# The experts' first layer in three fp32r products per weight tile, transposed as it is computed

## What is computed

```python
logits = xf @ gate_w + gate_b
top_w, top_i = jax.lax.top_k(logits, K)              # E, K, HID = 8, 2, 1024
gw = jax.nn.softmax(top_w, axis=-1)
combine = (gw[:, :, None] * jax.nn.one_hot(top_i, E)).sum(axis=1)
for e in range(E):
    h = jax.nn.gelu(xf @ w1[e] + b1[e], approximate=False)
    out = out + combine[:, e:e + 1] * (h @ w2[e] + b2[e])
shared = jax.nn.gelu(xf @ ws1 + bs1, approximate=False) @ ws2 + bs2
```

## Time and profile before

| | us |
|---|---|
| median of 3 runs | 805.07 (804.23 to 806.89) |
| the profiled execution | 804.36 |
| its span, first to last instruction | 802.6 |
| PE busy in the span | 742.9 (93%) |
| ACT, DVE, POOL busy | 331.6, 405.8, 218.7 |
| first hidden of the experts to the end of the last output | 460.8 to 778.2 |

### The profile page before, as it was taken

How to read it: one execution, slowest core, us unless ns; L and a number is a source line. 1 busy time by engine, 2 the same in 40 slices (tenths; PEclk the granted TensorE clock), 3 DMA queues, 4 the chain that set the end, 5 groups by cost and what they waited for, 6 DMA issues and landing times. The chain is left out here.

```text
span 802.6 us, 14818 instructions
## 1 busy us (share of the span) xinstructions
PE 742.9 (93%) x4804; PEld 563.6 (70%) x4805; DVE 405.8 (51%) x807; ACT 331.6 (41%) x885; POOL 218.7 (27%) x217
## 2 busy tenths in 40 slices
PE   6689999999999999999999899999999999999960
PEld 5567666967696766669999856767676767676740
DVE  3767788787879766667875321212121212121214
ACT  1232556456636654463332124343434343434324
POOL 5762212151214103002078201212121212121223
PEclk9987999999999999999999999999999999999985
DMA  9952331405050713032133499412121212121216
GB/s 289 250 152 54 56 110 40 84 27 148 0 108 0 226 29 55 7 134 88 63 114 112 95 318 311 96 27 40 26 39 26 39 26 39 26 39 26 27 15 215
DMA packets 60489, 71.76 MB, mean 89 GB/s; under 512 B 15264, under 2 KB 49952, under 8 KB 59552
## 3 DMA queue, kind: packets, MB, share of 16 engines
q1 hardware_dynamic: 47968, 57.03, 25.8%
q0 software_dynamic: 7152, 9.34, 7.1%
q10 hardware_dynamic: 5328, 4.85, 2.2%
HBM read 45.57 MB, written 25.11 MB: 88 GB/s over the span
## 5 line engine op out<-in xcount | busy, mean ns | idle before, releaser
L815 ACT ACTIVATE hT<-ps,b1T 128x128 f32<-128x128 f32 x312 | 84.8, 383 | 167.2 <-PE ps L1820 167.1
L1829 PE MATMUL ps<-we,hT 128*128 x624 | 142.9, 383 | 2.5 <-ACT hT L815 2.5
L1809 PE MATMUL ps<-we,xT 128*128 x312 | 140.5, 593 | 0.3 <-issue 0.3
L1829 PEld LDWEIGHTS ps<-we,hT 128*128 128x128 f32 x624 | 117.0, 192 | 17.6 <-issue 3.2
L1330 DVE COPY hp<-ps 128x512 f32<-128x512 f32 x78 | 50.3, 686 | 146.5 <-PE ps L1809 146.5
L1103 DVE TENSOR_REDUCE mx<-ps 128x4 f32<-128x512 f32 (+1 forms) x128 | 103.6, 819 | 20.6 <-PE ps L1627 19.4
L1809 PEld LDWEIGHTS ps<-we,xT 128*128 128x128 f32 x312 | 56.3, 191 | 56.4 <-issue 56.4
L726 ACT ACTIVATE pT<-ps 128x256 f32<-128x256 f32 x128 | 49.1, 384 | 69.7 <-PE ps L1643 59.5
L1627 PE MATMUL ps<-k_stack,q_stack 96*128 96x256 f32 (+1 forms) x256 | 72.3, 368 | 5.2 <-DVE mx L1103 3.0
L592 POOL CAST yidx<-meta 128x1 int32<-128x1 f32 x39 | 7.2, 184 | 234.8 <-ACT yw L824 234.8
L597 POOL DMA_INDIRECT row_sum<-yw,yidx x39 | 60.9, 1560 | 30.5 <-issue 26.4
(11 more groups left out here) (238 smaller groups left out, 1083.7 us busy)
## 6 DMA issues: line engine op xcount, KB each, us to landing
we<-in_w SPq DMA_DIRECT2D x16, 1024.0 KB, 8.9
k_stack<-k_rows SPq DMA_DIRECT2D x24, 256.0 KB, 4.8
slot_rows<-attn SPq DMA_DIRECT2D x1, 4992.0 KB, 24.5
xs<-slot_rows ACTq DMA_DIRECT2D x37, 128.0 KB, 2.0
k_rows<-k_s SPq DMA_DIRECT2D x16, 256.0 KB, 2.1
q_stack<-q_rows SPq DMA_DIRECT2D x48, 64.0 KB, 5.6
x_raw<-in_xT SPq DMA_DIRECT2D x4, 512.0 KB, 5.1
XW<-in_x SPq DMA_DIRECT2D x4, 512.0 KB, 8.5
```

The lines of the kernel that those rows point to most:

```text
L815: last = nc.scalar.activation(hT[:, c, :], ps[:, 4 + c // 4, (c % 4) * P:(c % 4 + 1) * P], ACT.Gelu, bias=b1T[:, bass.ds(e * NH + c, 1)])
L1809: m = nc.tensor.matmul(ps[:, 2 + c, :], xT[:, q, k, :], w[:, bass.ds(e, 1), k * HID + c * 512:k * HID + (c + 1) * 512].rearrange("p o n -> ...
L1829: m = nc.tensor.matmul(ps[:, 6, 0:D], hT[:, c, :], w[:, bass.ds(e, 1), KD * HID + c * D:KD * HID + (c + 1) * D].rearrange("p o n -> p (o n)"),
```

## The change

Hidden is turned round: chunks of the expert's weights stand (128 hidden units at a time), the tokens move, and the result comes out with hidden units as rows, as `gelu` needs it. Each of 8 chunks x 2 k takes the three fp32r products of `mm3`, of 128 columns each. `h_out`, `hp` and `turn_h` are gone. The high and low parts of the weights are made anew for each tile: `high` on ACT (2 copies of 128x1024) and `low` on DVE (2 differences of 128x1024), into one of two fixed homes by the tile's parity, three tiles ahead. The tokens get a low part too (`x_lo` on DVE). The result goes to banks 2 and 3 or 4 and 5 by parity, and `hT` is double. `home_even` lies over the raw shared weights, `home_odd` over `XW`; so `shared_y` moves to a ring of two chunks (`KEPT`), X is added ahead of the result (`y_in`), SP stores chunk 5 ahead of its wait for the scatters, and POOL stores the last chunk itself. The diff, cut:

```diff
+KEPT = 2
...
+        over = ExitStack()
+        home_odd = sb("home_odd", [P, 2, KD * HID], FR, over)
+        over.close()
...
+        home_even = sb("home_even", [P, 2, KD * HID], FR, over)
+        over.close()
         ws = sb("ws", [P, EW], F, mo)
...
-        xT = sb("xT", [P, 2, KD, P], F, mo)
-        hp = sb("hp", [P, HID], F, mo)
-        hT = sb("hT", [P, NH, P], F, mo)
+        sb("xT_was", [P, 2, KD, P], F, mo)
+        hT = sb("hT", [P, 2, NH, P], F, mo)
         ysum = sb("ysum", [P, 2, D], F, mo)
         yw = sb("yw", [P, 2, D], F, mo)
-        shared_y = ws[:, :].rearrange("p (t d) -> p t d", d=D)
         yidx = sb("yidx", [P, 2, 1], I32, mo)
...
+        xT = sb("xT", [P, 2, 2, KD, P], FR, mo)
+        shared_y = sb("shared_y", [P, 2 * KEPT, D], F, mo)
...
             def rows_kept(c):
                 sp.wait_ge(s["sy_out"], c + 1)
                 sp.dma_start(row_sum[bass.ts(c, CT), :].rearrange("(n p) d -> p n d", p=P),
-                             shared_y[:, bass.ds(2 * c, 2), :]).then_inc(s["kept_out"], 16)
-
-            for c in range(CHUNKS - 3):
+                             shared_y[:, 2 * (c % KEPT):2 * (c % KEPT) + 2, :]).then_inc(s["kept_out"], 16)
+
+            for c in range(CHUNKS - 2):
                 rows_kept(c)
             for q in range(4):
                 sp.wait_ge(st_sent[q], 16 * 2 * T // P // 4)
             for q in range(2):
                 sp.dma_start(xs[:, q, :], slot_rows[q * P:(q + 1) * P, 0:D]).then_inc(xs_in[q], 16)
             sp.dma_start(meta[:, :, :], slot_rows[:, D:].rearrange("(i p) m -> p i m", p=P)).then_inc(s["meta_in"], 16)
-            rows_kept(CHUNKS - 3)
             rows_kept(CHUNKS - 2)
             sp.wait_ge(s["sy_ps"], CHUNKS)
             for e in range(EARLY, E):
                 if e % EARLY == 0:
                     sp.wait_ge(s["we_in"], 32 * e)
                 load_expert(e)
-                if e == EARLY:
-                    rows_kept(CHUNKS - 1)
 
             for q in range(2):
                 sp.wait_ge(yw_sent[q], 16 * ((TILES + 1 - q) // 2))
...
-            pool.wait_ge(s["kept_out"], 16 * CHUNKS)
+            pool.wait_ge(s["sy_out"], CHUNKS)
+            pool.dma_start(row_sum[(CHUNKS - 1) * CT:CHUNKS * CT, :].rearrange("(n p) d -> p n d", p=P),
+                           shared_y[:, 2 * ((CHUNKS - 1) % KEPT):2 * ((CHUNKS - 1) % KEPT) + 2, :]).then_inc(s["last_kept"], 16)
+            pool.wait_ge(s["kept_out"], 16 * (CHUNKS - 1))
+            pool.wait_ge(s["last_kept"], 16)
...
                     if reused:
                         act.wait_ge(s["h_ps"], t - 1)
                     act.wait_ge(s["xT_ps"], t + 1)
-                    copy(xT[:, q, :, :], ps[:, 7 * q, 0:KD * P].rearrange("p (k t) -> p k t", k=KD), "xT_out")
+                    copy(xT[:, q, 0, :, :], ps[:, 7 * q, 0:KD * P].rearrange("p (k t) -> p k t", k=KD), "xT_out")
...
 
+                def high(t, q):
+
+                    e = table_expert(t) - 1
+                    if isinstance(t, int) and t < 2:
+                        if t:
+                            for st in st_sent:
+                                act.wait_ge(st, 16 * 2 * T // P // 4)
+                            act.wait_ge(s["sy_sum"], CHUNKS)
+                        else:
+                            act.wait_ge(s["ws_split"], 4)
+                    else:
+                        act.wait_ge(s["h_ps"], t - 1)
+                    act.wait_ge(s["we_in"], (e // EARLY) * (32 * EARLY) + 32 * EARLY)
+                    for k in range(KD):
+                        cols = slice(k * HID, (k + 1) * HID)
+                        copy((home_even, home_odd)[q][:, 0, cols],
+                             we[:, bass.ds(e, 1), cols].rearrange("p o n -> p (o n)"), "w_hi")
+
                 def gelu(t, q):
                     e = table_expert(t)
-                    act.wait_ge(s["hT_ps"], t + 1)
+                    act.wait_ge(s["h_ps"], t + 1)
+                    if not (isinstance(t, int) and t < 2):
+                        act.wait_ge(s["y_ps"], t - 1)
                     for c in range(NH):
-                        last = nc.scalar.activation(hT[:, c, :], ps[:, 4 + c // 4, (c % 4) * P:(c % 4 + 1) * P],
+                        last = nc.scalar.activation(hT[:, q, c, :], ps[:, 2 + 2 * q + c // 4, (c % 4) * P:(c % 4 + 1) * P],
                                                     ACT.Gelu, bias=b1T[:, bass.ds(e * NH + c, 1)])
                     last.then_inc(s["hT_out"], 1)
...
                         x_out(t + 2, q)
                     if not isinstance(t, int) or t + 1 < TILES:
                         gelu(t + 1, 1 - q)
+                    if not isinstance(t, int) or t + 3 < TILES:
+                        high(t + 3, 1 - q)
                     weight(t, q)
 
+                high(0, 0)
+                high(1, 1)
                 x_out(0, 0, False)
                 x_out(1, 1, False)
                 gelu(0, 0)
+                high(2, 0)
                 step(0, 0)
                 step(1, 1)
...
 
+            def kept_rows(c):
+                return shared_y[:, 2 * (c % KEPT):2 * (c % KEPT) + 2, :]
+
+            def y_in(c):
+                if c:
+                    dve.wait_ge(s["kept_out"], 16 * min(c, CHUNKS - 2))
+                nc.vector.tensor_tensor(kept_rows(c), X[:, 2 * c:2 * c + 2, :], b2b[:, 0:1, :].broadcast_to([P, 2, D]), ALU.add)\
+                    .then_inc(s["sy_sum"], 1)
+
             def y_out(c):
                 dve.wait_ge(s["sy_ps"], c + 1)
-                rows = shared_y[:, 2 * c:2 * c + 2, :]
-                nc.vector.tensor_tensor(rows, ps[:, Y_BANK[c], :].rearrange("p (n d) -> p n d", n=2),
-                                        b2b[:, 0:1, :].broadcast_to([P, 2, D]), ALU.add).then_inc(s["sy_sum"], 1)
                 dve.wait_ge(s["sy_sum"], c + 1)
-                nc.vector.tensor_tensor(rows, rows, X[:, 2 * c:2 * c + 2, :], ALU.add).then_inc(s["sy_out"], 1)
+                nc.vector.tensor_tensor(kept_rows(c), ps[:, Y_BANK[c], :].rearrange("p (n d) -> p n d", n=2),
+                                        kept_rows(c), ALU.add).then_inc(s["sy_out"], 1)
 
...
+            y_in(0)
             y_out(0)
...
+            y_in(1)
             y_out(1)
...
                     x_split(c + 2)
+                y_in(c - 1)
+                if c == CHUNKS - 1:
+                    y_in(c)
                 y_out(c - 1)
 
             def expert_tiles(table_expert):
-                def h_out(t):
-                    dve.wait_ge(s["h_ps"], t + 1)
-                    if not (isinstance(t, int) and t == 0):
-                        dve.wait_ge(s["hT_ps"], t)
-                    for c in range(2):
-                        last = nc.vector.tensor_copy(hp[:, c * 512:(c + 1) * 512], ps[:, 2 + c, :])
-                    last.then_inc(s["h_out"], 1)
+                def x_lo(t, q):
+                    dve.wait_ge(s["xT_out"], t + 1)
+                    lo_of(xT[:, q, 1, :, :], ps[:, 7 * q, 0:KD * P].rearrange("p (k t) -> p k t", k=KD),
+                          xT[:, q, 0, :, :], "xT_lo")
+
+                def low(t, q):
+                    e = table_expert(t) - 1
+                    home = (home_even, home_odd)[q]
+                    for k in range(KD):
+                        cols = slice(k * HID, (k + 1) * HID)
+                        dve.wait_ge(s["w_hi"], 2 * t + k + 1)
+                        lo_of(home[:, 1, cols], we[:, bass.ds(e, 1), cols].rearrange("p o n -> p (o n)"),
+                              home[:, 0, cols], "w_lo")
 
...
+                low(0, 0)
+                low(1, 1)
+                x_lo(0, 0)
+                x_lo(1, 1)
                 y_out(CHUNKS - 1)
-                h_out(0)
+                low(2, 0)
                 for t in range(2):
-                    h_out(t + 1)
+                    x_lo(t + 2, t)
                     y_sum(t, t, False)
+                    low(t + 3, 1 - t)
                 with dve.Fori(1, 1 + LOOPS) as i:
                     for q in range(2):
-                        h_out(2 * i + q + 1)
-                        y_sum(2 * i + q, q, True)
+                        t = 2 * i + q
+                        x_lo(t + 2, q)
+                        y_sum(t, q, True)
+                        low(t + 3, 1 - q)
                 for t in range(REST, TILES):
-                    if t + 1 < TILES:
-                        h_out(t + 1)
+                    if t + 2 < TILES:
+                        x_lo(t + 2, t % 2)
                     y_sum(t, t % 2, True)
+                    if t + 3 < TILES:
+                        low(t + 3, 1 - t % 2)
...
             def shared_output(c):
                 if c >= 2:
-                    pe.wait_ge(s["sy_sum"], c - 1)
+                    pe.wait_ge(s["sy_out"], c - 1)
...
                     if not (isinstance(t, int) and t < 2):
-                        pe.wait_ge(s["xT_out"], t - 1)
+                        pe.wait_ge(s["xT_lo"], t - 1)
...
```

(87 more changed lines are left out.)

## The result

The changed kernel takes 850.48 us (four runs: 851.52, 849.58, 840.06, 851.38) where the kernel before takes 805.59 beside it: a ratio of 1.0531, 95% interval 1.0493 to 1.057. It is slower, as forecast, and the 850.5 lies in the range of 828 to 860; the forecast was 841.5, so 9 us are missing from the sum. The profiled execution is one of 851.52, span 849.8.

The account below looks back on a forecast made before the run. PE alone was taken to set the pace of the expert tiles, 7.983 us each. Start +1.3, tiles +39.5 and end -4.1 sum to +36.7 us on 804.36, 841.1 (841.8 against the median), stated as 841.5; range 828 to 860.

Parts of the forecast that it names:

- p: Pace of one weight load and 128-column product in hidden, taken as 0.112 us; 48 per tile, break-even at 0.092.
- 0.067 (the load hides): In every tile's hidden, loads go in behind the running product: total -47.6, 757.5 us; chance 0.09.
- 0.120: In hidden, the 256-column pace is the floor of a load and product pair: +51.6, 856.7 us; chance 0.10.
- The tiles: From output(0) to output(37), 37 steps of 1.068 us more each: +39.5 us.
- Splits and new waits: In the tile loop, ACT's and DVE's added work and the ring's new waits cost nothing, a tile taking 9.05 us.
- The start: Ahead of hidden(0), DVE's added work costs 0; from hidden(0) to output(0) 10.97 us instead of 9.66, +1.3.
- a limit of 0.4 for the chain: Ahead of hidden(0), DVE's sums, differences and x_lo stay covered unless they take over 0.4 us more.
- the clock falls in hidden: PE waiting on loads lowers the clock and outputs' 3.45 us double; in all tiles 135 more, 976; chance 0.03.
- the prediction's own signs of being wrong: In the tiles: p not 0.11, PE waiting for DVE's w_lo, or the clock's row under 1.00.
- The end: Last two outputs: gap of 1.16 us saves 2.35, last product at full clock 1.78 more, together -4.1 us.
- The sum: Whole kernel: 1.3 + 39.5 - 4.1 = +36.7 us, so 841.1 for the profiled execution, 841.8 against the median.
- the range's upper end: Whole kernel: 860 us, taking in the 0.120 case and a mild ring wait.

Follow-up runs that it names:

- after_again: The changed kernel unaltered, run again on another chip: 877.14 us, 1.0609 of the kernel before.
- no_split: Changed kernel with the weights' high and low parts made for tiles 0 and 1 only, later tiles reusing them: 880.35 us, single run.
- fp32_stand: Changed kernel with one plain fp32 product in place of three fp32r ones, no low parts: 770.34 us, 0.9553 of the kernel before.
- tokens_stand: Changed kernel with tokens standing and weights moving, h's copy and transposes back, x_lo ahead of low(1): 804.56 us, ratio 0.971; again 776.51, 0.9627.

## Why the prediction was right, and where it was short

- **p.** Taken as 0.112, measured 0.112 from load to load, and 9.007 us a tile against 9.05. (Within the tile, output to hidden takes 3.27 where 3.45 was put, and hidden 5.50 where 5.38 was put; behind another hidden it takes the 5.38.) It came from the loads ahead of one-column products and behind the mask; the mask's next matmul, noted 0.06 later, was indeed no pace. The rivals of p, 0.067 (the load hides) and 0.120, both fall. The Trainium skill's rule for a load ("TensorE: Matmul & The Clock Gate", section "LDWEIGHTS (loading the stationary operand)"), 107 ns for 128 columns, is within 5% of this at full clock; its 81 ns for sustained pairs at 128 columns (section "Back-to-back issue gap") does not hold for these four-byte weights, which take 112.
- **The tiles.** +39.5 forecast from output(0) to output(37). Measured: (816.35 - 481.05) - (765.64 - 470.48) = +40.1, of which 2.3 is the first step's clock (11.30 us instead of 9.01). Without it +37.8, 1.7 under the forecast, which is the 0.04 a tile of the point above.
- **Splits and new waits cost nothing.** Right: without the splits a tile takes 9.006.
- **The start** is the step that failed. "All of it ends behind the last shared output ... so hidden(0) still starts at 460.5 to 460.9. I put 0 there." DVE's chain itself was reckoned well: 7.7 us from its last split of h (452.75) to x_lo's end (460.4), measured 462.4 - 455.7 = 6.7. But I set it against PE's end in the trace before, where the last shared output starts 0.7 us behind that split's end and is drawn out to 7.04 us by a lower clock. In the changed kernel it starts 0.8 ahead of the split's end (454.85 against 455.68) and takes 6.00: 2.6 us less cover, and the chain stuck out by 1.7. Most of that is not the change's doing. The whole shared expert runs 2.9 us later in this execution, and 2.2 of these are there from the first attention stage on: the transposes that start at 30.00 in the kernel before start at 32.17, while `after_again`, the same program, has them at 30.48. PE made up for part of it, since its wait for the token rows shrank from 2.30 to 0.94. DVE's chain moved by all of it (452.75 to 455.68). I had named a limit of 0.4 for the chain, and priced what lies beyond at itself. The runs show that a gap of 1.7 there costs 11.5 in the trace, 1.7 for itself and 9.8 for the clock behind it; between medians, where the gap is 2.2, it is 10.5.
- From hidden(0) to output(0) the forecast was 10.97; it took 18.52 in the profiled execution and 10.98 where the gap was closed.
- **The clock.** The prediction gave "the clock falls in hidden" 0.03, and held "full clock all through the attention stages" against it. That was a misreading: the trace of the kernel before has a granted clock of 0.84 from 40 to 60 us and 0.75 from 60 to 80. The clock did fall, in the hiddens of tiles 0 and 1 only, and so met one of the prediction's own signs of being wrong.
- **The end.** The gap forecast at 1.16 was 1.00, and the clock stayed up: 821.02 - 816.35 = 4.67 between the last outputs where 4.62 was forecast, and 3.72 for the last. Right, in size too.
- **The sum.** 841.1 for the profiled execution, measured 851.5. The 10.4 between them are +1.7 for the gap, +7.5 to output(0), +0.6 in the tiles (+2.3 of clock, -1.7 of pace), and some +0.6 at the end and behind it. That the median of 850.5 still lies in the range is partly luck: the range's upper end stood for p = 0.120, which did not come true, and not for a fall of the clock. The third run of the changed kernel took 840.06, at a mean clock of 0.974 where the others have 0.959 to 0.962. That fits an execution without the fall; its trace was not kept, so this is argued, not shown.

## What to carry to other kernels

Count weight loads before columns: at full clock a 128x128 load of four-byte weights took 0.112 us whether 128 or 64 columns followed, so three fp32r products with 128 columns each (0.336) cost more than the one plain fp32 product of two passes (0.224). Give each load 256 to 512 columns (0.120 and 0.239 a pair here), or let the product be the plain one. And where a change puts new work of another engine between two dense stretches of PE, reckon the gap against PE's own earliest time, not against a trace in which PE was held up. With 128-column products behind it, a gap of 1.7 us cost 11.5.

## What the runs showed of the hardware

- The weight load follows the granted clock: 0.112 us a load at 2.4 GHz, 0.21 at 1.2 GHz.
- With 64 columns behind each load the granted clock was 0.81 in the mean over the tiles, in a PE that never idled; with 128 it was 1.00. Behind a gap of some 2 us it fell with 128 columns, and stayed up in the one trace with 256. Once down in two hiddens in a row, it came back only in the first output product, some 20 us later; in the kernel before it fell too, at about 452.5 at the end of the gap of 2.30 (its last shared output took 7.04 us instead of 5.92), and was back at 1.00 from 456 on.
- POOL's one-column copy of the row numbers takes six times as long when it falls into DVE's forming of differences from SBUF. In the changed kernel the copy at 606.57 lasts until 607.72, and DVE's two differences from 605.31 until 607.67. The rows of the copy, first of the kernel before, then of the changed one, then of `no_split`:

```profile
L592 POOL CAST yidx<-meta x39: 184/184/187, 477.8 to 779.2; 128x1 int32<-128x1 f32 x39
```

```profile
L599 POOL CAST yidx<-meta x39: 184/1145/1151, 488.3 to 826.0; 128x1 int32<-128x1 f32 x39
```

```profile
L599 POOL CAST yidx<-meta x39: 183/185/188, 517.2 to 854.7; 128x1 int32<-128x1 f32 x39
```

  The numbers are minimum, median and maximum in ns. It is DVE's work and not ACT's copies beside it: `fp32_stand`, which keeps those copies and has no differences, has a median of 184. `tokens_stand` has both, but its copies start after the differences have ended, and has 185. Here it costs nothing, since POOL has time.
